# A graph-attention layer's preparation rewritten: plain fp32 projection, moments on VectorE, scores spread by DMA

## The chip, the cores and the metric

One NeuronCore of a Trainium2 chip runs the whole kernel. The metric is device time in microseconds (us), lower is better. The kernel before takes 437.5 us (median of 3 runs, 437.46 to 437.55).

Engine names as in the profile: PE is TensorE (matmul), PEld its weight loads, DVE is VectorE, ACT is ScalarE, POOL is GpSimd, SP is the queue that issues DMAs. Each engine runs its own instructions in order and waits on semaphores for the others.

## What is computed

```python
# x [4096, 256] f32, adj [4096, 4096] int32 (0.4 % ones), W1 [256, 256], b1, a1, a2 [256], b2 scalar
h   = relu(layernorm(x))                     # mean and variance of each row, eps 1e-5, no affine part
g   = h @ W1 + b1
e   = leaky_relu((g @ a1)[:, None] + (g @ a2)[None, :] + b2, 0.2)
att = softmax(where(adj > 0, e, -1e12), axis=1)
out = x + elu(att @ g)
```

The kernel never forms `e`. It uses exp(leaky(s1 + s2)) = exp(s2)·max(exp(s1 part), exp(s2 part)), so a weight is a maximum of two factors: R, which depends on the row i and is wanted along the free axis and repeated on all 128 partitions, and p, which depends on the neighbour j and sits one number per partition. A third factor u = exp(s2 - max) scales the rows of g.

## The kernel before

**Preparation.** The 4096 nodes are 32 tiles of 128, handled in 8 groups of 4 tiles (`GT`). For each group: `statistics` (4 `bn_stats` on VectorE), `moments` (7 tiny operations on GpSimd that turn them into mean and variance), `root` (ScalarE, square root), `invert` (VectorE, reciprocal and shift), `normalise` (2 of the 4 tiles on ScalarE, 2 on VectorE, into `xn`), `transposes` (8 on TensorE into PSUM banks 0 and 1), `relu_T` (ScalarE, PSUM to `hnT`, with a running sum in `hs`), `low_T` (VectorE, the rounding rest of `hnT`), `project` (TensorE: `W_hi·hnT + W_lo·hnT + W_hi·hnT_lo` in the fast fp32r format, 24 passes a group, into banks 2 to 5), `keep_h` (VectorE, PSUM plus bias to `h_raw`, in two halves). `exponents` (GpSimd) makes the arguments of the exponentials. For R, `repeat_s1` (ScalarE) repeats a group's 4 columns 128 times each, `spread` (TensorE) transposes them into PSUM banks 6 and 7, `keep_s` (ScalarE) copies them to R, and `exp_R` (ScalarE) takes the exponential 1024 columns at a time, one piece in each chunk of the main loop.

After the last group the maximum of s2 over all nodes is found (VectorE, TensorE, VectorE, TensorE, VectorE), `u` is made on ScalarE, the first two tiles of `hp_hi` and `hp_lo` follow, and TensorE starts the main loop. A small term `h_tiny`, 2^-100 times the sum of all h, is put into each accumulator by one matmul against `ones64` (`start_sum`), which covers rows with no neighbour.

**Main loop.** 4 chunks of 1024 output rows (8 PSUM banks of 128), each over 16 pairs of 128-node tiles. A pair is 1 MB of adjacency by DMA, then `sign` (ScalarE), `mask` (VectorE, two operations: max(R, p) times the sign), `high` (ScalarE, rounds to `w_hi`), `low` (VectorE, the rest `w_lo`), and 48 matmuls on TensorE: 32 of `w_hi` against `hp_hi` and `hp_lo`, then 16 of `w_lo` against `hp_hi`. In the first chunk the pairs' `hp_hi`, `hp_lo` are made on the way (`scale_h`, `round_h` on ScalarE, `low_h` on VectorE).

**What sets the order.** The instruction streams are written out by hand, one function for each engine, and meet at semaphores. Each engine's order around the change is the loop over `g` in its function. Two places are used by the prediction: VectorE's first `mask(0, 0, 0)`, which stands between two `keep_h`, and ScalarE's switch from the square-root table to the exponential table, which stands in front of its first exponential.

Of the kernel before, what the change touches and what calls it, by code (L numbers as in the profile page):

```python
# [32 lines left out]
P = 128  # L33
N = 4096
# [11 lines left out]
NORM_ACT = 2  # L46
# [6 lines left out]
EARLY = 6 * GT  # L53
# [27 lines left out]
def build(nc, adj_t, x, W1, vectors, out):  # L81
# [8 lines left out]
    with ctx:  # L90
# [37 lines left out]
        W_hi = sb("W_hi", [P, KC, HW], fp32r)  # L128
# [22 lines left out]
        cr = sb("cr", [P, TILES])  # L151
        cp = sb("cp", [P, TILES])
# [3 lines left out]
        H0, S0 = 2, 6  # L156
# [7 lines left out]
        pool_l = sem("pool_l")  # L164
        stat_ready = sem("stat_ready")
# [16 lines left out]
        s_kept = sem("s_kept")
# [10 lines left out]
        R_ready = sem("R_ready")  # L193
# [3 lines left out]
        eps_ready = sem("eps_ready")  # L197
        hp_tile = sem("hp_tile")
# [30 lines left out]
        def _(sp):  # L229
# [15 lines left out]
            for g in range(GROUPS):  # L245
                load_nodes(g)
                if g == 3:
                    load_adj(0, 0)
            for s in range(1, SLOTS):
                load_adj(s, s)  # L250

# [32 lines left out]
        def _(pool):  # L284
# [5 lines left out]
            links = [0]  # L290

            def link(ins):

                links[0] += 1
                ins.then_inc(pool_l, 1)
                pool.wait_ge(pool_l, links[0])

            def moments(g):

                pool.wait_ge(stat_ready, g + 1)  # L300
                st, mo = stats[:, g, :, :], mom[:, g, :, :]
                pool.tensor_tensor(mo[:, 0, :], st[:, :, 1], st[:, :, 4], ALU.add)
                pool.tensor_tensor(mo[:, 1, :], st[:, :, 1], st[:, :, 4], ALU.subtract)
                link(pool.tensor_tensor(mo[:, 2, :], st[:, :, 2], st[:, :, 5], ALU.add))
                pool.tensor_scalar(mean[:, g * GT:(g + 1) * GT], mo[:, 0, :], 0.5, None, ALU.mult)
                pool.tensor_tensor(mo[:, 3, :], mo[:, 1, :], mo[:, 1, :], ALU.mult)
                link(pool.tensor_scalar(mo[:, 2, :], mo[:, 2, :], 4.0 / F, None, ALU.mult))
                pool.tensor_tensor(var[:, g * GT:(g + 1) * GT], mo[:, 3, :], mo[:, 2, :], ALU.add).then_inc(var_ready, 1)

# [8 lines left out]
            for g in range(4):  # L318
                moments(g)
            pool.wait_ge(g3_ready, 1)  # L320
            for g in range(GROUPS):
                if g + 4 < GROUPS:
                    moments(g + 4)
                exponents(g)

# [7 lines left out]
        def _(act):  # L333
            act.dma_start(W1x[:, :, 0:F], W1.rearrange("(c p) f -> p c f", p=P)).then_inc(w_in, 16)
            act.dma_start(vec[:, :], vectors.partition_broadcast(P)).then_inc(vec_in, 16)

            def root(g):

                act.wait_ge(var_ready, g + 1)
                act.activation(std[:, g * GT:(g + 1) * GT], var[:, g * GT:(g + 1) * GT], ACT.Sqrt,  # L340
                               scale=0.25, bias=eps[:, 0:1]).then_inc(std_ready, 1)

            def normalise(g):

                act.wait_ge(rstd_ready, g + 1)
                if g >= 2:
                    act.wait_ge(tp_ready, KC * (g - 1))
                for t in range(NORM_ACT):
                    tile = g * GT + t
                    last = act.activation(xn[:, g % 2, t, :], x_s[:, tile, :], ACT.Identity,  # L350
                                          scale=rstd[:, tile:tile + 1], bias=shift[:, tile:tile + 1])
                last.then_inc(xn_act, 1)

            def relu_T(g):
# [559 lines left out]
```

## Time and profile before

| | us |
|---|---|
| median of 3 runs | 437.5 |
| the profiled execution's own time | 437.48 |
| its span in the trace | 435.7 |
| PE busy | 412.5 (95 %) |
| VectorE busy | 377.1 (87 %) |
| ScalarE busy | 315.9 (73 %) |
| GpSimd busy | 23.0 (5 %) |
| PE busy in 0 to 20 us | 6.5 |
| PE busy in 70 to 400 us | all of it |

The page's slices, each a fortieth of the span (10.9 us):

```profile
PE   0689979999999999999999999999999999999995
DVE  3999899999999389999996299999991799999925
ACT  2678899999996298957763798859562989586512
POOL 2333200000000000000000000000000000000003
```

A digit is the busy share of a slice in tenths. The preparation is the first five and a half slices, up to about 58 us; TensorE has gaps there and none from the seventh slice on. A busy share says nothing by itself about what an engine is worth, so the rows below give single starts and durations. The span is 1.8 us shorter than the device time of the same execution; that difference lies outside the trace.

### The profile page before, as it was taken

The numbers are of one execution on the slowest core, as the hardware profiler recorded it, in microseconds if no ns is written. First come the engines' busy times: TensorE is split into PE (matmuls) and PEld (weight loads), VectorE is DVE, ScalarE is ACT, GpSimd is POOL, SyncE is SP. The second block draws the span as 40 slices with busy tenths as digits, with TensorE's granted clock in tenths as the row PEclk, the third lists the DMA queues.
The fourth block names the chain that finished last, engine by engine and source line by source line (L and its number), as shares of the span: only waits on it lengthen the run. The fifth ranks groups of instructions, "written<-read, shape, count | busy, mean of one in ns | idle before, by whom it ended". The sixth has DMA issues, their size and how long they took to land.

```text
span 435.7 us, 8648 instructions
## 1 busy us (share of the span) xinstructions
PE 412.5 (95%) x3399; PEld 409.1 (94%) x3399; DVE 377.1 (87%) x404; ACT 315.9 (73%) x312; POOL 23.0 (5%) x94
## 2 busy tenths in 40 slices
PE   0689979999999999999999999999999999999995
PEld 0688979999999999999999999999999999999995
DVE  3999899999999389999996299999991799999925
ACT  2678899999996298957763798859562989586512
POOL 2333200000000000000000000000000000000003
PEclk9999999999999999999999999999999999999999
DMA  8940015556555725638478155647477256476202
GB/s 271 385 178 1 0 45 211 193 213 211 193 193 194 289 93 205 235 145 261 173 254 308 68 193 200 249 152 263 154 265 259 73 219 213 174 243 238 98 0 98
DMA packets 22360, 80.68 MB, mean 185 GB/s; under 512 B 1472, under 2 KB 14016, under 8 KB 14144
## 3 DMA queue, kind: packets, MB, share of 16 engines
q1 hardware_dynamic: 21920, 79.70, 52.1%
q10 hardware_dynamic: 416, 0.66, 0.5%
q8 instruction: 16, 0.26, 0.2%
q14 instruction: 8, 0.07, 0.0%
HBM read 76.15 MB, written 4.19 MB: 184 GB/s over the span
## 4 chain that ended last, share of the span: by engine, by line
PE 88%; DVE 7%; ACT 2%; DMA 2%; issue 0%; SPq 0%; DVEq 0%; ACTq 0%
PE ps L604 51%; PE ps L606 25%; PE ps L622 2%; PE ps L623 2%; PE ps L624 2%; DVE stats L664 2%; DMA x_s<-x 2%; DVE hnT_lo L691 1%; PE ps L531 1%; DVE h_raw L700 1%; PE ps L533 1%; PE ps L532 1%; DVE xn L681 1%; PE ps L580 1%; PE ps L519 1%; ACT h_raw L439 1%
## 5 line engine op out<-in xcount | busy, mean ns | idle before, releaser
L604 PE MATMUL ps<-hp_hi,w_hi 128*128 (+1 forms) x944 | 229.8, 282 | 0.9 <-ACT w_hi L391 0.9
L606 PE MATMUL ps<-hp_lo,w_hi 128*128 (+1 forms) x944 | 229.7, 282 | 0.0
L738 DVE SCALAR_TENSOR_TENSOR adj_s<-R,p,adj_s 128x1024 f32<-128x1024 f32 x128 | 158.1, 1275 | 31.7 <-ACT adj_s L383 31.7
L604 PEld LDWEIGHTS ps<-hp_hi,w_hi 128*128 128x128 f32 x944 | 178.3, 189 | 1.2 <-ACT w_hi L391 1.1
L606 PEld LDWEIGHTS ps<-hp_lo,w_hi 128*128 128x128 f32 x944 | 178.1, 189 | 0.0
L748 DVE SCALAR_TENSOR_TENSOR w_lo<-adj_s,w_hi 128x2048 fp32r<-128x2048 f32 x64 | 146.0, 2282 | 0.4 <-ACT w_hi L391 0.3
L391 ACT ACTIVATE w_hi<-adj_s 128x2048 fp32r<-128x2048 f32 x64 | 122.4, 1912 | 29.8 <-DVE adj_s L738 29.5
L383 ACT ACTIVATE adj_s<-adj_s 128x2048 f32<-128x2048 int32 x64 | 122.3, 1912 | 23.2 <-DMA adj_s<-adj_t 23.0
L604 PE MATMUL ps<-hp_hi,w_lo 128*128 (+1 forms) x944 | 123.1, 283 | 0.6 <-DVE w_lo L748 0.6
L604 PEld LDWEIGHTS ps<-hp_hi,w_lo 128*128 128x128 f32 x944 | 117.4, 189 | 0.8 <-DVE w_lo L748 0.8
L455 ACT ACTIVATE y<-ps 128x258 f32<-128x258 f32 x24 | 9.3, 387 | 27.9 <-PE ps L624 27.9
L330 POOL TENSOR_TENSOR adj_s<-y,adj_s 128x256 f32<-128x256 f32 x7 | 4.8, 692 | 372.9 <-DVE y L886 372.9
L519 PE MATMUL ps<-ident,xn 128*128 128x128 f32 x64 | 10.2, 312 | 15.1 <-ACT xn L350 11.3
L519 PEld LDWEIGHTS ps<-ident,xn 128*128 128x128 f32 x64 | 8.5, 161 | 15.8 <-issue 11.5
L622 PE MATMUL ps<-hp_hi,w_hi 128*128 128x258 f32 x80 | 22.6, 282 | 0.0
L623 PE MATMUL ps<-hp_lo,w_hi 128*128 128x258 f32 x80 | 22.6, 282 | 0.0
L624 PE MATMUL ps<-hp_hi,w_lo 128*128 128x258 f32 x80 | 22.5, 282 | 0.0
L531 PE MATMUL ps<-W_hi,hnT 128*128 128x258 f32 x64 | 19.1, 299 | 0.8 <-DVE h_raw L700 0.6
L532 PE MATMUL ps<-W_lo,hnT 128*128 128x258 f32 x64 | 18.3, 287 | 0.0
L533 PE MATMUL ps<-W_hi,hnT_lo 128*128 128x258 f32 x64 | 18.3, 286 | 0.0
L664 DVE BATCH_NORM_STATS2 stats<-x_s 128x6 f32<-128x256 f32 x32 | 11.2, 411 | 6.0 <-DMA x_s<-x 6.0
L623 PEld LDWEIGHTS ps<-hp_lo,w_hi 128*128 128x128 f32 x80 | 15.1, 189 | 0.0
(90 smaller groups left out, 270.2 us busy)
## 6 DMA issues: line engine op xcount, KB each, us to landing
adj_s<-adj_t SPq DMA_DIRECT2D x64, 1024.0 KB, 4.8
x_s<-x SPq DMA_DIRECT2D x8, 512.0 KB, 10.4
o_s<-x SPq DMA_DIRECT2D x3, 1024.0 KB, 7.5
out<-o_s SPq DMA_DIRECT2D x6, 512.0 KB, 6.8
adj_s<-x SPq DMA_DIRECT2D x1, 1024.0 KB, 5.3
out<-adj_s SPq DMA_DIRECT2D x8, 128.0 KB, 1.7
vec<-vectors ACTq DMA_DIRECT2D x1, 384.5 KB, 6.4
W1x<-W ACTq DMA_DIRECT2D x1, 256.0 KB, 4.3
```

The costliest lines, as they stand in the source:

```text
L383: act.activation(adj_w[:, c, :, :], adj_s[:, c, :, :], ACT.Sign).then_inc(signed, 1)
L391: act.activation(w_hi[:, c, :, :], adj_w[:, c, :, :], ACT.Relu).then_inc(hi_ready, 1)
L519: last = pe.transpose(ps[:, kc, t * P:(t + 1) * P], xn[:, u, t, kc * P:(kc + 1) * P], ident[:, :])
L531: pe.matmul(acc, hnT[:, u, kc, node], W_hi[:, kc, :], start=kc == 0, stop=False)
L532: pe.matmul(acc, hnT[:, u, kc, node], W_lo[:, kc, :], start=False, stop=False)
L604: last = pe.matmul(acc, block_w, hh, start=False, stop=False)
L606: pe.matmul(acc, block_w, hl, start=False, stop=False)
L622: pe.matmul(acc, w_hi[:, b + k, s, col], hh, start=False, stop=False)
L623: pe.matmul(acc, w_hi[:, b + k, s, col], hl, start=False, stop=False)
L624: last = pe.matmul(acc, w_lo[:, b + k, s, col], hh, start=False, stop=end)
L738: last = dve.scalar_tensor_tensor(sgn, R[:, ds(ic * CW, CW)], p[:, ds(source(r, c) + s, 1)], sgn, ALU.max, ALU.mult)
L748: dve.scalar_tensor_tensor(w_lo[:, c, :, :], adj_w[:, c, :, :], 0.0, w_hi[:, c, :, :].bitcast(fp32), ALU.max, ALU.subtract).then_inc(lo_re ...
```

## The change

Constants: `NORM_ACT` 2 to 3 (ScalarE normalises 3 of 4 tiles, 2 in the first two groups), `XN = 4` buffers for `xn`, `EARLY` 24 tiles to 16, `WARM = 19`.

- **Loads.** W1 and the vectors move from ScalarE's queue to SP's, behind group 0 of x; the first adjacency tile moves behind all of x.
- **Moments.** GpSimd's 7 operations go; VectorE runs 4 `bn_aggr` a group.
- **Projection.** `W_hi`, `W_lo`, `hnT_lo`, `split_weights` and `low_T` go. `project` is 8 plain fp32 matmuls a group. Transposes alternate between banks 0, 1 and 6, 7.
- **R.** `repeat_s1`, `spread`, `keep_s`, `exp_R` go. The scores are transposed once (8 tiles, then 24) into rows of PSUM, copied (`copy_r`), exponentiated as 8x128 and 24x128 (`exp_r`), written to a DRAM buffer and read back repeated on all partitions by DMA.
- **Start.** 19 fp32 matmuls of `ones` against `ones` ahead of the first transposes.
- **Tiny sums.** `start_sum` ahead of chunk 0 and at each chunk's start becomes `add_tiny` in the chunk's last pairs; the number of them is the same. `first_tile` opens the accumulators with `hp_hi` alone, then `hp_lo`.
- **Order of the first pairs.** On VectorE `low` of pair 0 stands ahead of `mask` of pair 1, and the first `mask` stands behind group 5 instead of behind group 6.

```diff
 # sync
-            for g in range(GROUPS):
+            load_nodes(0)
+            sp.dma_start(W1x[:, :, 0:F], ...); sp.dma_start(vec[:, :], ...)
+            for g in range(1, GROUPS):
                 load_nodes(g)
-                if g == 3:
-                    load_adj(0, 0)
+            load_adj(0, 0)
...
+            def spread(k):
+                a, b = R_PART[k]
+                sp.wait_ge(r_ready, k + 1)
+                sp.dma_start(r_rows[tiles, :], r_row[k][:, :]).then_inc(r_out, 16)
+                sp.wait_ge(r_out, (k + 1) * 16)
+                sp.dma_start(R[:, a * P:b * P],
+                             r_rows[tiles, :].rearrange("t p -> (t p)").partition_broadcast(P)).then_inc(R_in, 16)
 # scalar
+            def exp_r(k):
+                act.wait_ge(r_copied, k + 1)
+                act.activation(r_row[k][:, :], r_row[k][:, :], ACT.Exp).then_inc(r_ready, 1)
...
+            for g in range(2, GROUPS):
                 if g + 1 < GROUPS:
                     relu_T(g + 1)
                 if g + 3 < GROUPS:
                     root(g + 3)
+                    normalise(g + 3)
+                if g == 3:
+                    sign(0, 0, 0)
+                if g == 5:
+                    exp_r(0)
                     act.wait_ge(c_ready, EARLY // GT)
                     act.activation(p[:, 0:EARLY], cp[:, 0:EARLY], ACT.Exp).then_inc(p_ready, 1)
+                if g == 6:
+                    sign(0, 0, 1)
                     high(0, 0, 0)
+            exp_r(1)
 # tensor
+            def keep_warm(n):
+                for _ in range(n):
+                    pe.matmul(ps[:, H0 + GT - 1, 0:P], ones[:, :], ones[:, :], start=True, stop=True)
...
                     for kc in range(KC):
-                        pe.matmul(acc, hnT[:, u, kc, node], W_hi[:, kc, :], start=kc == 0, stop=False)
-                        pe.matmul(acc, hnT[:, u, kc, node], W_lo[:, kc, :], start=False, stop=False)
-                        last = pe.matmul(acc, hnT_lo[:, u, kc, node], W_hi[:, kc, :], start=False, stop=kc == KC - 1)
+                        last = pe.matmul(acc, hnT[:, g % 2, kc, node], W1x[:, kc, :], start=kc == 0, stop=kc == KC - 1)
...
+            transposes(0); project(0); transposes(1); project(1); transposes(2); project(2); transposes(3)
+            for g in range(3, GROUPS):
+                if g + 1 < GROUPS:
+                    transposes(g + 1)
+                if g == 4:
+                    turn_r(0)
+                project(g)                      # group 7: sum_h() after its second tile
+                if g == 4:
+                    pe.wait_ge(r_copied, 1)
 # vector
+                for t in range(GT):
+                    dve.bn_aggr(agg[:, g, t, :], stats[:, g, t, :]).then_inc(agg_ready, 1)
...
+            for g in range(2, GROUPS - 1):
+                if g + 3 < GROUPS:
+                    statistics(g + 3)
+                keep_h(g, (0,))
+                if g + 3 < GROUPS:
+                    invert(g + 3)
+                    normalise(g + 3)
                 if g == 4:
+                    copy_r(0)
+                keep_h(g, (1,))
+                if g == 5:
                     dve.wait_ge(p_ready, 1)
+                    dve.wait_ge(R_in, 16)
                     mask(0, 0, 0)
```

The order of VectorE's instructions around the first mask, before. `hnT_lo` is `low_T`, `h_raw` is `keep_h`, `hsrep` the repeated sums, `adj_s` the mask; the `h_raw` ahead of the mask is group 6, the one behind it group 7.

```order
L691 SCALAR_TENSOR_TENSOR hnT_lo<-ps,hnT 128x512 [waits hn_ready]
L700 TENSOR_TENSOR h_raw<-ps,b1x 128x516 [waits h_ready] x2
L782 TENSOR_REDUCE hsum<-hs 128x2 [waits hn_ready]
L784 TENSOR_SCALAR hsrep<-ones,hsum 128x128 [waits dve_c]
L784 TENSOR_SCALAR hsrep<-ones,hsum 128x128
L738 SCALAR_TENSOR_TENSOR adj_s<-R,p,adj_s 128x1024 [waits signed,R_ready,p_ready]
L738 SCALAR_TENSOR_TENSOR adj_s<-R,p,adj_s 128x1024
L700 TENSOR_TENSOR h_raw<-ps,b1x 128x516 [waits h_ready] x2
L792 TENSOR_REDUCE gm<-h_raw 128x1 [waits h_kept]
```

The same engine and place in the changed kernel. The three `h_raw` ahead of the mask are the second half of group 4 and both halves of group 5; the two behind it are group 6.

```order
L691 TENSOR_TENSOR h_raw<-ps,b1x 128x516 [waits h_ready]
L672 RECIPROCAL rstd<-std 128x4 [waits std_ready]
L673 SCALAR_TENSOR_TENSOR shift<-agg,rstd 128x4 [waits dve_c]
L682 TENSOR_SCALAR xn<-x_s,agg,rstd 128x256 [waits tp_ready]
L741 COPY r_row<-ps 8x128 [waits rT_ready]
L691 TENSOR_TENSOR h_raw<-ps,b1x 128x516 [waits h_ready] x3
L724 SCALAR_TENSOR_TENSOR adj_s<-R,p,adj_s 128x1024 [waits signed,R_in,p_ready]
L724 SCALAR_TENSOR_TENSOR adj_s<-R,p,adj_s 128x1024
L691 TENSOR_TENSOR h_raw<-ps,b1x 128x516 [waits h_ready] x2
L777 TENSOR_REDUCE hsum<-hs 128x2 [waits hn_ready]
```

The mask moved one group forward, and it now waits for `R_in`, the count of a DMA.

ScalarE in the changed kernel, from its last square root to the work behind the exponentials; `std` is `root(7)`, the two `hnT` pairs are `relu_T(6)` and `relu_T(7)`.

```order
L340 ACTIVATE std<-agg,eps 128x4 [waits agg_ready]
L349 ACTIVATE xn<-x_s,shift,rstd 128x256 [waits tp_ready,rstd_ready]
L349 ACTIVATE xn<-x_s,shift,rstd 128x256 x2
L359 ACTIVATE hnT,hs<-ps 128x512 [waits tp_ready,h_ready]
L359 ACTIVATE hnT,hs<-ps 128x512 [waits tp_ready]
L365 ACT_TABLE_LOAD
L365 ACTIVATE r_row<-r_row 8x128 [waits r_copied]
L406 ACTIVATE p<-cp 128x16 [waits c_ready]
L359 ACTIVATE hnT,hs<-ps 128x512 [waits tp_ready,h_ready]
L359 ACTIVATE hnT,hs<-ps 128x512 [waits tp_ready]
L370 ACTIVATE adj_s<-adj_s 128x2048 [waits adj_in1]
L378 ACTIVATE w_hi<-adj_s 128x2048 [waits masked]
```

The table switch and the first exponential stand behind `relu_T(6)`; before, they stood behind `relu_T(7)` and a `repeat_s1`, and R needed no DMA.

## Rows read from the trace of the kernel before

**Rows 1.** The page's chain of work that ended last, shares by engine.

```profile
PE 88%; DVE 7%; ACT 2%; DMA 2%; issue 0%; SPq 0%; DVEq 0%; ACTq 0%
```

**Rows 2.** Windows: stretch, length, busy us and instructions of PE, PEld, DVE, ACT, POOL.

```profile
70.00:80.00 10.00, 10.00 (x85) 10.00 (x85) 9.67 (x8) 10.00 (x12) 0.00 (x0) 1.00 0.54 197
```

**Rows 3.** Timeline of PE, end of preparation: start, us, instruction, idle before.

```profile
52.74 1.03 PE L568 MATMUL ps<-W1x,hsrep 128*128 128x256 f32 x4
53.60 0.60 PE L543 MATMUL ps<-ident,s1rep 128*128 128x128 f32 x4
...
65.68 0.39 PE L604 MATMUL ps<-hp_hi,w_hi 128*128 128x258 f32 x1 [0.88 <-ACT w_hi L391]
```

**Rows 4.** Timeline of PE, the first groups.

```profile
11.35 1.94 PE L519 MATMUL ps<-ident,xn 128*128 128x128 f32 x8 [11.35 <-ACT xn L350]
...
17.00 0.56 PE L531 MATMUL ps<-W_hi,hnT 128*128 128x258 f32 x1
...
22.32 1.07 PE L519 MATMUL ps<-ident,xn 128*128 128x128 f32 x8 [1.59 <-DVE xn L681]
```

**Rows 5.** Timeline of VectorE, one whole group in mid-preparation.

```profile
28.81 0.17 DVE L671 RECIPROCAL rstd<-std 128x4 f32<-128x4 f32 x1
...
29.09 1.29 DVE L691 SCALAR_TENSOR_TENSOR hnT_lo<-ps,hnT 128x512 fp32r<-128x512 f32 x2
30.30 0.73 DVE L681 TENSOR_SCALAR xn<-x_s,mean,rstd 128x256 f32<-128x256 f32 x2
30.94 1.40 DVE L664 BATCH_NORM_STATS2 stats<-x_s 128x6 f32<-128x256 f32 x4
32.26 1.28 DVE L700 TENSOR_TENSOR h_raw<-ps,b1x 128x516 f32<-128x516 f32 x2
```

**Rows 6.** Timeline of ScalarE, sign, relu_T, normalise and root.

```profile
31.40 1.90 ACT L383 ACTIVATE adj_s<-adj_s 128x2048 f32<-128x2048 int32 x1
33.20 0.58 ACT L360 ACTIVATE hnT<-ps 128x512 fp32r<-128x512 f32 x1
...
34.34 1.09 ACT L350 ACTIVATE xn<-x_s,shift,rstd 128x256 f32<-128x256 f32 x2
35.32 0.29 ACT L340 ACTIVATE std<-var,eps 128x4 f32<-128x4 f32 x1
```

**Rows 7.** Timeline of ScalarE, the table switch.

```profile
48.16 1.28 ACT L415 ACT_TABLE_LOAD   x1
49.45 0.22 ACT L415 ACTIVATE p<-cp 128x24 f32<-128x24 f32 x1
```

**Rows 8.** Timeline of VectorE, first mask and maximum.

```profile
50.82 2.48 DVE L738 SCALAR_TENSOR_TENSOR adj_s<-R,p,adj_s 128x1024 f32<-128x1024 f32 x2
...
54.54 0.21 DVE L792 TENSOR_REDUCE gm<-h_raw 128x1 f32<-128x32 f32 x1
```

**Rows 9.** Timeline of ScalarE, from the first hp_hi on.

```profile
56.54 0.91 ACT L433 ACTIVATE hp_hi<-h_raw,u 128x258 fp32r<-128x258 f32 x2
...
58.16 1.06 ACT L374 ACTIVATE R<-ps 128x512 f32<-128x512 f32 x2
59.26 0.64 ACT L446 ACTIVATE hp_hi<-h_raw 128x516 fp32r<-128x516 f32 x1
```

**Rows 10.** The page's costliest groups, one row: busy, mean ns, idle before.

```profile
L748 DVE SCALAR_TENSOR_TENSOR w_lo<-adj_s,w_hi 128x2048 fp32r<-128x2048 f32 x64 | 146.0, 2282 | 0.4 <-ACT w_hi L391 0.3
```

**Rows 11.** The page's DMA issues: KB each, median us to landing.

```profile
adj_s<-adj_t SPq DMA_DIRECT2D x64, 1024.0 KB, 4.8
...
out<-adj_s SPq DMA_DIRECT2D x8, 128.0 KB, 1.7
```

**Rows 12.** Timeline of VectorE, first statistics and weights.

```profile
5.32 1.41 DVE L664 BATCH_NORM_STATS2 stats<-x_s 128x6 f32<-128x256 f32 x4 [4.37 <-DMA x_s<-x]
...
10.64 0.28 DVE L707 COPY b1x<-vec 128x256 f32<-128x256 f32 x1
...
12.35 0.21 DVE L715 TENSOR_SCALAR W1x<-w1a 128x1 f32<-128x1 f32 x2
```

More of the change, by code:

```diff
@@ L45 @@
 GROUPS = TILES // GT
-NORM_ACT = 2
+NORM_ACT = 3
+PAIRED = 2
+WARM = 19
+XN = 4
+R_CUT = CW // P
+R_PART = ((0, R_CUT), (R_CUT, TILES))
 HW = F + 2
@@ L289, in _ @@
                                pattern=[[-1, P]], channel_multiplier=1).then_inc(pool_c, 1)
[L290 to L308, printed above, removed]
+            pool.memset(ones64[:, :].bitcast(fp32), 1.0 / 64).then_inc(h_sum_set, 1)
+            pool.memset(h_sum[:, F:F + 1], float(N)).then_inc(h_sum_set, 1)
+            pool.memset(h_sum[:, F + 1:HW], 0.0).then_inc(h_sum_set, 1)
             def exponents(g):
@@ L480, in round_of @@
                         sign(*ahead(ic, r, c, 2))
-                    if r is FIRST_ROUND and c == 2 and not last:
-                        exp_R(ic + 1)
                     if inner and not first and c in (1, 2):
@@ L564, in _, with turn_r @@
-            project(GROUPS - 1, 1)
-            pe.wait_ge(hsrep_ready, 1)
-            for kc in range(KC):
-                last = pe.matmul(ps[:, 0, 0:F], hsrep[:, kc, :], W1x[:, kc, 0:F], start=kc == 0, stop=kc == KC - 1)
-            last.then_inc(hsum_ps, 1)
-            spread(GROUPS - 2, 0)
+                    if g == GROUPS - 1 and t == 1:
+                        sum_h()
+            def turn_r(k):
+                a, b = R_PART[k]
+                pe.transpose(ps[0:b - a, RB[k], 0:P], cr[:, a:b], ident[:, :]).then_inc(rT_ready, 1)
@@ new lines, in sum_h @@
+            def sum_h():
+                pe.wait_ge(hsrep_ready, 1)
+                for kc in range(KC):
+                    last = pe.matmul(ps[:, 0, 0:F], hsrep[:, kc, :], W1x[:, kc, 0:F], start=kc == 0, stop=kc == KC - 1)
+                last.then_inc(hsum_ps, 1)
+            pe.wait_ge(pool_c, 1)
+            keep_warm(WARM)
+            pe.wait_ge(pool_c, 3)
+            transposes(0)
+            pe.wait_ge(w1x_ready, 1)
+            project(0)
+            transposes(1)
+            project(1)
@@ L587, in pair @@
                     for s in range(2):
+                        if first and begin and part == 0 and s == 0:
+                            first_tile()
+                            continue
                         if first and part == 0:
@@ L804, in _ @@
-            rest = slice(P // 2, P)
-            dve.wait_ge(tiny_ready, 1)
-            dve.scalar_tensor_tensor(h_tiny[rest, :], h_sum[rest, :], TINY, h_tiny[rest, :].bitcast(fp32),
-                                     ALU.mult, ALU.subtract).then_inc(prep_done, 1)
+            dve.wait_ge(hn_ready, GROUPS * KC)
+            link(dve.reduce_sum(hsum[:, :], hs[:, :, :], AX.X))
+            for kc in range(KC):
+                last = dve.tensor_scalar(hsrep[:, kc, :], ones[:, :], hsum[:, kc:kc + 1], None, ALU.mult)
@@ L839, in round_of @@
                     end = last and r is LAST_ROUND
-                    if not (end and c == SLOTS - 1):
+                    begin = first and r is FIRST_ROUND and c == 0
+                    if not (end and c == SLOTS - 1) and not begin:
                         mask(*ahead(ic, r, c, 1))
                     low(ic, r, c)
+                    if begin:
+                        mask(*ahead(ic, r, c, 1))
                     if first and not (r is LAST_ROUND and c == SLOTS - 1):
                         low_h(*ahead(ic, r, c, 1)[1:])
+                    if first and r is FIRST_ROUND and c == 2:
+                        tiny()
                     if r is FIRST_ROUND and c == 3 and not first:
```

321 lines of the change are left out of this document (141 added, 180 removed).

## The prediction, made before the changed kernel was run

> **What bounds the kernel now.** I read the chain of waits first: 88 % of it is TensorE [rows 1]. Then the windows by time: from 70 us on TensorE is busy in all of every stretch, at 85 matmuls in 10 us, which is 0.118 us each [rows 2]. Then TensorE's own timeline for the last place where it waits: pair 1 of the first chunk starts at 65.68 after 0.88 us of idle [rows 3]. Behind that point nothing but TensorE counts, and its matmuls are the same in both kernels. So the change is worth what it moves the start of pair 1, plus any matmul that it moves from ahead of that point to behind it. I call the end of the last projection X. It is 52.74 before, where the sum of h starts directly behind it [rows 3], and pair 1 starts 12.94 later.
>
> **Costs of the parts, per group.** The plain fp32 projection: the two fp32 matmuls of the h sum leave four records, 0.86 us from their start to the next instruction [rows 3], so 0.215 a record and 0.43 a matmul of 256 columns. A group has 8: 3.44 us. Before it had 24 passes at 0.118: 2.83. With eight transposes (0.9; their rows say 1.07 with the last one's tail [rows 4]) TensorE needs 4.3 us a group. VectorE before: starts at 28.81, 29.09, 30.30, 30.94, 32.26 and 1.2 for the last give 4.65 a group [rows 5]. It loses low_T (1.21) and one of two xn (0.32) and gains four bn_aggr and a link. No row shows bn_aggr. The nearest are tiny operations: 0.06 to 0.10 each as the second of two in a row (12.35, two in 0.21 [rows 12]), 0.17 busy as a reciprocal [rows 5]. That bounds four and a link between 0.3 and 0.8; I take 0.45, near the short end because the four do not wait for each other. VectorE: 3.6. ScalarE: two relu_T 1.14, root 0.2, three xn at 0.5 each [rows 6]: 2.85. By these sums TensorE would set the pace at 4.3. The order says otherwise, so I walk it.
>
> **The walk.** P0 to P7 are the starts of the eight projections. x's first group: 5.32 before [rows 12]; now no other load shares its first microsecond, so 4.6 (bounds 4.0 and 5.3). Statistics, bn_aggr, root, reciprocal, shift: 7.2. ScalarE's two xn: 8.3. Transposes 8.5 to 9.4, at the fast level: the 19 fp32 matmuls of ones end shortly before. Before, the first eight took 1.94 and later ones 1.07 [rows 4]; that halving is 1.2 against 2.4 GHz. The weights take VectorE 1.9 (10.64 to 12.35 plus 0.21 [rows 12]) and end at 9.7; relu_T(0) ends at 10.4. P0 = 10.5, against 17.00 before [rows 4]: 6.5 us ahead.
>
> P1 = 16.1: P0 ends at 14.0, transposes of group 1 only then, relu_T behind them.
> P2 = 23.2, not 20.4. P1 ends at 19.55, the transposes at 20.45, relu_T(2) on ScalarE at 21.5; root(3) stands behind it (21.8), VectorE waits for that root before keep_h(1), and P2 needs the banks that keep_h(1) frees (0.6 for reciprocal and xn, 0.7 for the half). TensorE idles 2.8.
> P3 = 30.1, not 27.5. VectorE has from 23.65: statistics and moments of 4 (1.8), root (0.35), invert and xn (0.6), the scalars (1.2: two of the four reductions of rows 12 and two linked tiny operations), statistics of 5 (1.8), a half of keep_h(2) (0.65), in all 6.4.
> P4 = 34.7. P3 ends at 33.6, one set of transposes.
> P5 = 40.7, not 39.1. ScalarE from 34.0: three xn 1.5, sign 1.8, relu_T(5) 1.2, root(7) 0.3, so VectorE's invert(7), xn and copy_r(0) end at 39.7, and the next transposes wait for that copy.
> ScalarE goes on: xn(7) to 40.75, relu_T(6) to 41.95, the table switch 1.3 to 43.25 [rows 7], exp_r to 43.5.
>
> **The new wait.** R's first columns now come over two DMAs in a row. The write of 4 KB: 1.7, as the 128 KB stores [rows 11]. The repeated read of 512 KB: the 1 MB load takes 4.8 [rows 11]; two points on a line, 128 KB in 1.7 and 1024 KB in 4.8, give 3.0, and I add 0.2 for 128 repeats: 3.2 (bounds 2.4, half of 4.8, and 4.8). R is in at 48.5. VectorE has been standing in front of mask(0,0,0) since keep_h(5) at 45.0. Queued behind it: the mask, 2.4 [rows 8], then keep_h(6), for whose banks the last projection waits. TensorE ends P6 at 48.5 and starts P7 at 48.5 + 0.05 + 2.4 + 0.7 = 51.65. The wait and the mask thus cost TensorE 3.1 us. Counted from P5 it is tight: relu_T(6) 1.25, table 1.3, exp 0.25, two DMAs 4.9, mask and half 3.1 give P5 + 10.9, while TensorE alone could start P7 at P5 + 7.8.
> P7 takes 3.44 and the h sum in its middle 0.86: X = 55.95, against 52.74.
>
> The Trainium skill, "ScalarE: Activation LUTs", section "What ACT_TABLE_LOAD costs", puts a switch at about 2.66 us, a load of 1283 ns and a drain of 1380 ns. The trace agrees with the load (1.28) and not with the drain: the next activation starts 1.29 after the load's start [rows 7]. By the page's rule R would be in 1.4 us later, and the time 441.0; I go by the row.
>
> **From X to pair 1.** The maximum starts at X + 0.45, now straight from PSUM; before, the first mask and both halves of keep_h held it until 54.54 [rows 8], X + 1.8. From the maximum to the first hp_hi it was 2.00 (54.54 to 56.54 [rows 8, 9]); the same steps remain, so X + 2.45. From there to pair 1 ScalarE took 9.14 (56.54 to 65.68 [rows 3, 9]). It loses two copies to R, 1.10 (58.16 to 59.26 [rows 9]), and gains a tiny exponential, 0.2: 8.2, so X + 10.7. VectorE gets there at about the same time by the other way: keep_h(7) to X + 3.2, two hp_lo 0.9, low 2.2 [rows 10], mask 2.4 [rows 8], then high 1.9: X + 10.9, since low now stands ahead of the mask. I take 10.9. Low of pair 0 is thereby early, which buys nothing by itself: TensorE waits for pair 1's high all the same.
> Pair 1 starts at 55.95 + 10.9 = 66.85, 1.15 later than before. Eight tiny matmuls of chunk 0 that stood in waiting time ahead of pair 1 now stand in the saturated stretch: 8 × 0.118 = 0.95. From there on the work for pairs 2 to 4 comes 0.5 us or more ahead of TensorE by the same durations, and the second read of R, 1.5 MB ahead of the adjacency loads in SP's queue, is wanted only at the chunk's end.
>
> **Sum.** 437.48 (the profiled execution, 435.7 of span and 1.8 outside; the median is 437.50, the same) + 1.15 + 0.95 = 439.6. The 6.5 us won at P0 go to: P2 2.8, P3 2.6, P5 1.6, R's wait 3.1, and the slower fp32 projection.
>
> **Rivals.**
> A. The early groups run at TensorE's own pace: ScalarE and VectorE catch up, no stall at P2, P3, P5. Then P5 = 10.5 + 1.2 + 5 × 4.3 = 33.2, P7 = 44.1, X = 48.4, pair 1 at 59.3: 437.5 - 6.4 + 0.95 = 432.1. For it: VectorE's sum of 3.6 is below 4.3. Against it: the root behind relu_T is a circle through three engines, and rows 5 show before that VectorE in order is what sets the pace.
> B. The other side, by R's trip: place, the wait in front of mask(0,0,0). If both DMAs together take 1.7 instead of 4.9, R is in by 45.2, the stall shrinks from 3.6 to nothing, X = 52.75 and pair 1 starts at 63.65: 437.5 - 2.0 + 0.95 = 436.4. Equality with before is reached at a trip of 2.8. For it: the write is only 4 KB. Against it: no DMA in the rows lands in under 1.7, and there are two, one waiting for the other.
> C. The clock. TensorE has gaps of 2.8 (ahead of P2) and 3.1 (ahead of P7), longer than the 1.59 ahead of a fast burst [rows 4]. If it falls to 1.2 GHz there, a projection takes up to 3.4 more, some of which the R wait absorbs: 439.6 + 1 to 4, so about 442. The Trainium skill, "TensorE: Matmul & The Clock Gate", says the clock is halved after an idle stretch and given back by sustained work; the trace agrees in that the first work ran at half speed. None of the rows shows a fast engine falling back after a gap of this length.
> D. bn_aggr at its long bound, 0.35 more in each of seven groups on VectorE's path: 2 later, 441.7.
>
> **How the numbers follow.** My walk with small errors 0.48, A 0.08, B (a short trip, or the walk too slow by 2 to 4 in front) 0.17, C 0.15, D 0.12. No change within what a measurement can tell is 0.2 %, 0.9 us: 436.6 to 438.4. Faster: A, B's larger part and a little of the walk: 0.23. Same: a part of the walk and of B: 0.17. Slower: 0.60. The range leaves A out below and the worst of C above: 436.2 to 442.8. The likeliest case alone: 438.3 to 441.
>
> **What the next profile would show.** Right: P0 at 10 to 11; a gap on TensorE of 2 to 3 ahead of P2; VectorE idle about 3.5 in front of the first mask, released by a DMA; no idle of TensorE behind pair 1; pair 1 at 66 to 67. Wrong: no idle at the mask (then B), TensorE without gaps from P1 to P5 (then A), transposes of 1.9 us after P1 (then C). The whole forecast falls if TensorE idles anywhere behind pair 1, or if fp32 passes take other than 0.215.

## The result, and the profile after

The changed kernel took a median of 441.53 us (eight runs, 439.45 to 443.24) against 437.56 for the kernel before (437.43 to 437.68): 1.0085 times the time [1.0063, 1.0106], so 4.0 us slower. The forecast was 439.6 with a range to 442.8: the sign is right, the range holds, and the value is 1.9 short. It lies outside the narrower interval of the likeliest case (438.3 to 441). The spread is new too: single executions lay 3.8 us apart, against 0.25 before.

The profiled execution took 442.08, and one subtraction tells where the time is. Pair 1 starts at 69.17 instead of 65.68 [rows 3]: 3.49 later. From its start to the end of the span it is 371.13 instead of 370.02: 1.11 more. 437.48 + 3.49 + 1.11 = 442.08. TensorE has no idle time behind that start up to 400 us, as before [rows 2]; windows, columns as there but for TensorE alone (length, busy and matmuls, granted clock, DMA share, GB/s):

```profile
100.00:400.00 300.00, 300.00 (x2504) 1.00 0.59 205
```

So everything of interest lies ahead of 69.17. The page's chain answers to [rows 1]; its clock line has a dip in the second tenth of the span, and none behind it:

```profile
PE 87%; DVE 4%; ACT 4%; DMA 3%; issue 1%; SPq 0%; DVEq 0%; ACTq 0%
PEclk9999889999999999999999999999999999999999
```

TensorE's timeline answers to [rows 3, 4]: start, us, instruction, and in brackets the idle time ahead and what ended it. L517 with 16 records is one group's projection. P0 is the row at 10.76; of P6 and P7 see the rows at 45.08 and 52.47.

```profile
10.76 3.75 PE L517 MATMUL ps<-W1x,hnT 128*128 128x258 f32 x16 [1.60 <-DVE W1x L706]
16.37 3.75 PE L517 MATMUL ps<-W1x,hnT 128*128 128x258 f32 x16 [0.92 <-ACT hnT L359]
...
23.59 3.73 PE L517 MATMUL ps<-W1x,hnT 128*128 128x258 f32 x16 [2.59 <-DVE h_raw L691]
30.41 3.72 PE L517 MATMUL ps<-W1x,hnT 128*128 128x258 f32 x16 [1.14 <-DVE h_raw L691]
...
39.78 1.09 PE L505 MATMUL ps<-ident,xn 128*128 128x128 f32 x8 [1.18 <-DVE r_row L741]
40.71 3.65 PE L517 MATMUL ps<-W1x,hnT 128*128 128x258 f32 x16
...
45.08 3.65 PE L517 MATMUL ps<-W1x,hnT 128*128 128x258 f32 x16
...
52.47 3.55 PE L517 MATMUL ps<-W1x,hnT 128*128 128x258 f32 x8 [3.74 <-DVE h_raw L691]
55.82 1.18 PE L532 MATMUL ps<-W1x,hsrep 128*128 128x256 f32 x4
56.84 1.90 PE L517 MATMUL ps<-W1x,hnT 128*128 128x258 f32 x8
...
69.17 0.39 PE L604 MATMUL ps<-hp_hi,w_hi 128*128 128x258 f32 x1
```

Read the brackets from top to bottom. P0 really is 6.2 us ahead of before, and P1 even 7.4 (23.80 before). The brackets ahead of P2 (2.59), P3 (1.14) and the transposes for P5 (1.18) take most of that back, and the largest one, 3.74, ahead of P7, takes the rest and more. Before, in the same places, two starts to compare with:

```profile
28.44 0.36 PE L531 MATMUL ps<-W_hi,hnT 128*128 128x258 f32 x1 [0.22 <-DVE h_raw L700]
...
49.78 0.36 PE L531 MATMUL ps<-W_hi,hnT 128*128 128x258 f32 x1
```

The first is P2, the second P7: the changed kernel is 4.9 us ahead at the one and 2.7 behind at the other. Read then the second column of the two halves of P7: eight records take 3.55 in the first half and 1.90 in the second. That is the clock (columns as above; the granted clock, the third number, is the share of TensorE's full speed, 1.00 for 2.4 GHz and 0.50 for 1.2):

```profile
49.00:52.00 3.00, 0.00 (x0) 1.00 0.00 0
52.00:54.00 2.00, 1.53 (x4) 0.68 0.00 0
54.00:56.00 2.00, 2.00 (x6) 0.50 0.00 0
56.00:58.00 2.00, 2.00 (x11) 0.97 0.00 0
```

TensorE stood idle to 52.47, fell from 2.4 to 1.2 GHz as it began again, and had nearly the full clock again in the last of these windows. The projection's first half pays 1.65 for it, and the h sum's start the rest.

VectorE's timeline around the new wait, where [rows 8] had the first mask start at 50.82:

```profile
44.40 0.70 DVE L691 TENSOR_TENSOR h_raw<-ps,b1x 128x516 f32<-128x516 f32 x1 [1.05 <-PE ps L517]
49.24 2.48 DVE L724 SCALAR_TENSOR_TENSOR adj_s<-R,p,adj_s 128x1024 f32<-128x1024 f32 x2 [4.13 <-DMA R<-r_rows]
51.63 1.29 DVE L691 TENSOR_TENSOR h_raw<-ps,b1x 128x516 f32<-128x516 f32 x2
```

VectorE is done with group 5 at 45.1, stands 4.13 us in front of the mask, and only behind the mask comes `keep_h(6)`, whose banks P7 needs. The chain in order of time (start, us, what) shows what it waits for: the switch to the exponential's table, the exponential of R's row, and the two transfers one behind the other:

```profile
42.00 1.28 ACT L365
...
43.29 0.32 ACT r_row L365
...
43.62 1.22 DMA r_rows<-r_row
...
44.86 4.28 DMA R<-r_rows
```

### The profile page after: what moved, and what is told of

It is laid out like the page before. It is cut to its first block, busy times and chain, and to the rows that moved or that the text cites. A ratio compares the mean times of both kernels' runs of the same rounds, so it can differ in the third digit from the quotient of the medians.

```text
span 440.3 us, 8443 instructions
## 1 busy us (share of the span) xinstructions
PE 420.8 (96%) x3343; PEld 413.1 (94%) x3343; DVE 367.8 (84%) x415; ACT 308.9 (70%) x300; POOL 10.7 (2%) x39
## 4 chain that ended last, share of the span: by engine, by line
PE 87%; DVE 4%; ACT 4%; DMA 3%; issue 1%; SPq 0%; DVEq 0%; ACTq 0%
PE ps L604 51%; PE ps L606 25%; PE ps L517 3%; PE ps L625 2%; PE ps L624 2%; PE ps L626 2%; DMA vec<-vectors 2%; ACT hnT L359 1%; DMA R<-r_rows 1%; DVE stats L663 1%; PE ps L566 1%; DVE h_raw L691 1%; ACT adj_s L370 1%; DVE adj_s L724 1%; ACT h_raw L423 1%
## 5 line engine op out<-in xcount | busy, mean ns | idle before, releaser
L604 PEld LDWEIGHTS ps<-hp_hi,w_hi 128*128 128x128 f32 x936 | 177.6, 190 | 0.3 <-ACT w_hi L378 0.3
L604 PEld LDWEIGHTS ps<-hp_hi,w_lo 128*128 128x128 f32 x944 | 117.4, 189 | 0.0
L517 PE MATMUL ps<-W1x,hnT 128*128 128x258 f32 x128 | 31.4, 398 | 10.0 <-DVE h_raw L691 7.5
L517 PEld LDWEIGHTS ps<-W1x,hnT 128*128 128x128 f32 x128 | 24.5, 196 | 14.8 <-issue 8.3
L624 PEld LDWEIGHTS ps<-hp_hi,w_hi 128*128 128x128 f32 x80 | 15.1, 189 | 0.0
L626 PEld LDWEIGHTS ps<-hp_hi,w_lo 128*128 128x128 f32 x80 | 15.1, 189 | 0.0
L489 ACT ACTIVATE y<-ps,rden 128x256 f32<-128x256 f32 x8 | 3.8, 474 | 15.6 <-DVE rden L883 15.6
L349 ACT ACTIVATE xn<-x_s,shift,rstd 128x256 f32<-128x256 f32 x22 | 11.7, 591 | 3.9 <-DVE shift L673 3.9
```

The source lines that it names most:

```text
L349: last = act.activation(xn[:, g % XN, t, :], x_s[:, tile, :], ACT.Identity, scale=rstd[:, tile:tile + 1], bias=shift[:, tile:tile + 1])
L517: last = pe.matmul(acc, hnT[:, g % 2, kc, node], W1x[:, kc, :], start=kc == 0, stop=kc == KC - 1)
L604: last = pe.matmul(acc, block_w, hh, start=fresh, stop=False)
L624: pe.matmul(acc, w_hi[:, b + k, s, col], hh, start=False, stop=False)
L626: last = pe.matmul(acc, w_lo[:, b + k, s, col], hh, start=False, stop=end)
```

## The experiments

Nine more kernels were run beside the kernel before, which took 437.55 to 437.58 in all of them. Two numbers of each profile are used throughout: the start of pair 1, and the tail, from there to the end of the span.

### 1. The first mask behind the last projection's work (e1_mask_late)

The changed kernel, with the wait for R and the mask behind the h sum's operand, so behind `keep_h(6)`:

```diff
                 keep_h(g, (1,))
-                if g == 5:
-                    dve.wait_ge(p_ready, 1)
-                    dve.wait_ge(R_in, 16)
-                    mask(0, 0, 0)
...
             last.then_inc(hsrep_ready, 1)
+            dve.wait_ge(p_ready, 1)
+            dve.wait_ge(R_in, 16)
+            mask(0, 0, 0)
```

> The first mask and its wait for R move behind keep_h(6) and the repeated sums; nothing else changes. Theory 1 (the wait for R's two DMAs in front of keep_h(6) holds the last projection, and the clock that falls in that gap slows it): R lands at 49.2 as in the changed kernel, no gap of TensorE ahead of the last projection, it starts at 48.7 and all its passes run at the fast level, X = 53.0, pair 1 at 63.5, time 436 to 436.8. Theory 2 (the slower fp32 projection and the stalls of the early groups are the loss, the wait for R only covers other waits): pair 1 stays at 68 to 69 and the time at 440 to 442.

Measured: 436.92 (436.2 to 439.08, ten runs), 0.999 of before [0.9978, 1.0002]: no clear difference from before, and 4.6 us below the changed kernel. Pair 1 starts at 64.08, 5.1 earlier; the tail is 371.12, the same. TensorE's timeline, then VectorE's:

```profile
45.65 5.40 PE L517 MATMUL ps<-W1x,hnT 128*128 128x258 f32 x24
...
51.74 1.90 PE L517 MATMUL ps<-W1x,hnT 128*128 128x258 f32 x8
```

```profile
50.54 2.48 DVE L724 SCALAR_TENSOR_TENSOR adj_s<-R,p,adj_s 128x1024 f32<-128x1024 f32 x2
```

P7 follows P6 without a gap (24 records in one row), at the full clock, and the mask waits for nothing: R was in before it was wanted. The R trip itself is harmless here; what cost the time is the place of the wait for it. Of the 5.1 between the two profiles, 3.3 lie ahead of P7 (its start is 49.1 here, 52.47 there) and 1.8 between P7's start and X (4.3 here, 6.1 there), which is the clock.

One row of this profile has the low clock in an earlier place. P2 stands behind the same gap as in the changed kernel, with the same instructions ahead of it, and took 5.18 instead of 3.73:

```profile
23.53 5.18 PE L517 MATMUL ps<-W1x,hnT 128*128 128x258 f32 x16 [2.59 <-DVE h_raw L691]
```

Most of that disappeared in the stall ahead of P3; P5 was 0.6 later (41.28 instead of 40.71).

### 2. The gap filled, the wait kept (e2_gap_filled)

This parts the wait from the clock that fell behind it. The changed kernel with 16 matmuls of ones (32 records) while TensorE waits for P7:

```diff
+                if g == GROUPS - 1:
+                    keep_warm(16, 1)
                 project(g)
```

> 16 plain fp32 matmuls of ones (about 3.4 us at the fast level) into a free bank fill TensorE's gap ahead of the last projection; the wait for R stays. Theory 1 with the clock as a term of its own: the last projection starts at 52.5 as before, takes 4.3 in place of 6.1, X = 56.9, pair 1 at 67.4, time 440.0 to 440.6, and the runs lie closer together than the 3.8 us of the changed kernel. Theory 3 (the slow passes are not from the gap, or are hidden behind ScalarE anyway): 441 to 442, the same spread.

Measured: 440.48 (439.81 to 442.23, four runs), 1.0061 [1.0044, 1.0077], 1.05 below the changed kernel. The projection behind the filled gap is fast again, while VectorE still waits for R:

```profile
50.77 3.73 PE L496 MATMUL ps<-ones 128*128 128x128 f32 x32
54.34 1.91 PE L517 MATMUL ps<-W1x,hnT 128*128 128x258 f32 x8
```

```profile
50.66 2.48 DVE L726 SCALAR_TENSOR_TENSOR adj_s<-R,p,adj_s 128x1024 f32<-128x1024 f32 x2 [3.37 <-DMA R<-r_rows]
```

In the profiles this parts the two: X minus P7's start is 4.3 here and 6.1 in the changed kernel, so the slow clock at P7 was worth 1.8 in that execution, and the wait the rest. For the medians it does not: the intervals overlap ([1.0063, 1.0106] there), so the 1.05 is not shown to be more than noise. The filling also cost something of its own. P7 starts 3.68 behind the mask's start, 3.23 in the changed kernel, since the ones ran some 0.45 too long. The profiled execution was the slowest of the four, and it shows the same thing in other gaps that this kernel leaves open. Its first projection, behind a gap of 1.49, took 5.44 instead of 3.75, and P2 5.20 instead of 3.73; the windows have the clock at 0.66 and 0.69 there:

```profile
10.69 5.44 PE L517 MATMUL ps<-W1x,hnT 128*128 128x258 f32 x16 [1.49 <-DVE W1x L708]
...
25.14 5.20 PE L517 MATMUL ps<-W1x,hnT 128*128 128x258 f32 x16 [2.60 <-DVE h_raw L693]
```

```profile
10.00:15.00 5.00, 4.31 (x12) 0.66 1.10 362
...
25.00:30.00 5.00, 4.86 (x16) 0.69 0.46 190
```

### 3. The fp32 projection alone (e3_fp32_alone)

The kernel before, with only this:

```diff
-                        pe.matmul(acc, hnT[...], W_hi[:, kc, :], ...)
-                        pe.matmul(acc, hnT[...], W_lo[:, kc, :], ...)
-                        last = pe.matmul(acc, hnT_lo[...], W_hi[:, kc, :], ...)
+                        last = pe.matmul(acc, hnT[...], W1x[:, kc, :], start=kc == 0, stop=kc == KC - 1)
...
-            split_weights()
-            low_T(0)
```

> The kernel before with one part of the change alone: plain fp32 projection, no low_T, no split weights. Theory 1: VectorE loses 1.2 us a group and 1.1 at the start, TensorE gains 0.6 a group (0.9 + 3.44 + 0.44 for the spread = 4.8 against a pace of 4.65 before): the two cancel to 1 us, time 437 to 438.7. Theory 2 (the fp32 projection is the loss): 439.5 or more.

Measured: 437.89 (437.16 to 438.61, ten runs), 1.0005 [0.9995, 1.0015]: no difference. Pair 1 at 66.16, tail 370.04. The groups follow at 4.80:

```profile
27.20 3.65 PE L531 MATMUL ps<-W1x,hnT 128*128 128x258 f32 x16
...
32.00 3.65 PE L531 MATMUL ps<-W1x,hnT 128*128 128x258 f32 x16
```

VectorE's 4.65 a group became TensorE's 4.80 (the rows say 3.65 for 16 records at 0.215 each because the last record's tail is in them). Taking work off VectorE gave back nothing, since the same edit gave it to TensorE.

### 4. Without the warm-up (e4_no_warm)

`WARM = 19` to `WARM = 0` in the changed kernel.

> The changed kernel without the 19 matmuls of ones. Theory 1 (the chain P0, P1, root(3), keep_h(1), P2 passes every delay on): the first transposes take 1.9 in place of 1.1, P0's first passes 0.43 each in place of 0.22, P1 starts 2 to 3 later and so does all behind it, time 443 to 445. Rival: the 2.6 us gap ahead of P2 and the later ones absorb it, time within 1 us of the changed kernel's 441.5.

Measured: 443.01 (442.33 to 443.81, four runs), 1.013 [1.0113, 1.0147], 1.5 slower than the changed kernel, at the low edge of what was expected. The start runs at half speed:

```profile
8.32 1.94 PE L505 MATMUL ps<-ident,xn 128*128 128x128 f32 x8 [8.32 <-ACT xn L349]
11.13 5.60 PE L517 MATMUL ps<-W1x,hnT 128*128 128x258 f32 x16 [0.87 <-ACT hnT L359]
...
54.38 1.98 PE L517 MATMUL ps<-W1x,hnT 128*128 128x258 f32 x8 [2.93 <-DVE h_raw L691]
```

P0 is 1.9 longer and P5 2.7 later, but pair 1 in the profile only 0.2 later (69.40). Not all of the 2.7 is the missing warm-up: P2 took 5.13 here too, behind its gap of 2.59. The last row shows where the 2.7 went besides the wait: here P7 came out of a gap of 2.93 at full speed, where the changed kernel, behind 3.74, fell to half. The 0.2 is thus a matter of two single executions; the medians differ by 1.5.

### 5. The tiny matmuls left out (e5_tiny_out)

Experiment 1's kernel, without chunk 0's eight tiny matmuls; this leaves the tiny sum out of chunk 0.

```diff
-                    add_tiny(ib)
+                    if not first:
+                        add_tiny(ib)
```

> e1 with the eight tiny matmuls of chunk 0 left out (rows without a neighbour in the first 1024 lose their small term). The term of my sum: eight matmuls in the saturated stretch, 8 x 0.118 = 0.95 us less than e1, 435.9 to 436.2 by median. Rival: TensorE has slack there (ScalarE or VectorE sets the pace behind pair 1) and nothing changes: 436.9.

Measured: 435.82 (435.33 to 437.36, six runs), 0.9964 [0.9952, 0.9977]. The median is 1.1 below experiment 1's, and the tail, which the clock of the preparation can't touch, fell from 371.12 to 370.11. That is 1.0 of the 1.1 by which the tail had grown from before, so nothing else of the change costs more than 0.1 behind pair 1.

### 6. The front stalls taken out (e6_front_only)

The changed kernel; on VectorE `keep_h(1)` no longer stands behind the root of group 3 nor the scalars behind group 4's work, and on ScalarE the first sign stands behind the first exponentials:

```diff
             statistics(3)
+            scalars()
+            keep_h(1)
             invert(3)
             normalise(3)
-            keep_h(1)
             statistics(4)
...
-            scalars()
...
-                if g == 3:
-                    sign(0, 0, 0)
...
                     act.activation(p[:, 0:EARLY], cp[:, 0:EARLY], ACT.Exp).then_inc(p_ready, 1)
+                    sign(0, 0, 0)
```

> The changed kernel with three moves in the early groups and the mask where the change put it: keep_h(1) ahead of invert(3), the scalars into VectorE's 3 us wait for root(3), sign(0,0,0) from ahead of relu_T(5) to behind the first exponentials. Theory 1 (the stalls ahead of P2, P3 and P5 are order on VectorE and ScalarE, and everything behind P5 hangs on P5): P2 at 22.0, P5 at 37.2 in place of 40.7, the wait for R as long as before, time 438.0 (437.5 to 438.7). Rival (R's trip or another engine's sum is a floor of its own): 440 or more.

Measured: 437.4 (435.34 to 439.64, twelve runs), 0.9996 [0.9979, 1.0013], so 4.1 below the changed kernel and 0.1 below the expected range. P2 starts at 21.55 instead of 23.59, P5 at 36.77 instead of 40.71, pair 1 at 66.03. The profiled execution, 438.98, is 1.6 above the median. The wait for R is untouched, and in this execution the clock falls behind it:

```profile
44.75 2.48 DVE L723 SCALAR_TENSOR_TENSOR adj_s<-R,p,adj_s 128x1024 f32<-128x1024 f32 x2 [3.60 <-DMA R<-r_rows]
```

```profile
47.98 3.78 PE L516 MATMUL ps<-W1x,hnT 128*128 128x258 f32 x8 [3.20 <-DVE h_raw L690]
```

### 7. Both (e7_both)

Experiments 1 and 6 together.

> e1's mask and e6's three moves together. Theory 1: the two gains add, X = 49.5, pair 1 at 60, time 433.4 (432.8 to 434.2), below the kernel before by 4. Rival: R lands too late for the mask behind the repeated sums, and takes 1 to 3 us back: 434.5 to 436.5.

Measured: 432.73 (432.31 to 434.48, five runs), 0.9899 [0.9885, 0.9913]. The two gains add: 4.6 and 4.1 make 8.7, measured 8.8. Pair 1 starts at 59.39:

```profile
40.97 5.40 PE L516 MATMUL ps<-W1x,hnT 128*128 128x258 f32 x24
...
59.39 0.39 PE L603 MATMUL ps<-hp_hi,w_hi 128*128 128x258 f32 x1 [1.57 <-ACT w_hi L378]
```

Pair 1 is where rival A had it (59.3), but not by rival A's way. A had P5 at 33.2 and the wait for R left in, so P7 at 44.1; here P5 starts at 36.60, with gaps of about 1 ahead of P0, P1 and P2, and P7 follows P6 without a wait, at 44.5. That the two agree at pair 1 is chance.

### 8. And the other gaps filled (e8_gaps_filled)

Experiment 7's kernel with 6, 3, 5 and 6 matmuls of ones ahead of P0, P1, P2 and the first pair:

```diff
             transposes(0)
+            keep_warm(6)
             pe.wait_ge(w1x_ready, 1)
             project(0)
             transposes(1)
+            keep_warm(3, 1)
             project(1)
             transposes(2)
+            keep_warm(5, 7)
             project(2)
...
             def first_tile():
+                pe.wait_ge(r_copied, 2)
+                keep_warm(6, RB[1])
                 pe.wait_ge(hi_ready, 1)
```

> e7 with plain fp32 matmuls of ones in four gaps of TensorE: 6 ahead of P0, 3 ahead of P1, 5 ahead of P2, 6 ahead of the first pair (each about 0.22 us at the fast level). Theory 1 with the clock as the cause of the spread: fewer stretches at the half clock, spread of the runs under 1 us in place of 3, median lower than e7's by 0.2 to 0.6. Rival (the spread comes from elsewhere, or the fills push the real work back): the same spread, median equal or higher.

Measured: 432.5 (432.46 to 433.01, four runs), 0.9888 [0.9874, 0.9902]. The mean granted clock of the profiled execution is 1.000 and the runs lie 0.55 apart, where experiment 7's lie 2.2 and the changed kernel's 3.8. The median moved by 0.23 only, which is inside the intervals. Experiment 7's 2.2 is one execution of five: 434.48, at a mean granted clock of 0.990, where its other four have 0.996 to 0.999 and lie 0.6 apart. This fits the clock in the gaps ahead of pair 1 as a large part of the spread, and does not show it: four runs are few, and experiment 3's ten runs lie 1.45 apart at 0.999 to 1.000, so there is a source besides.

### 9. The tiny matmuls back into waiting time (e9_tiny_in_wait)

Experiment 8's kernel; `h_tiny` is made on GpSimd, and chunk 0's eight tiny matmuls stand ahead of pair 1:

```diff
+            pool.tensor_scalar(h_tmp[:, :], h_sum[:, :], TINY, None, ALU.mult)
+            pool.tensor_scalar(h_tiny[:, :], h_sum[:, :], TINY, None, ALU.mult).then_inc(tiny_ready, 1)
+            pool.wait_ge(tiny_ready, 1)
+            pool.tensor_tensor(h_tiny[rest, :], h_tmp[rest, :], ..., ALU.subtract).then_inc(prep_done, 1)
...
+                if m == 1:                      # ahead of pair 1
+                    for ib in range(BANKS):
+                        add_tiny(ib)
```

> e8 with chunk 0's eight tiny matmuls moved into TensorE's wait of 1.6 us ahead of pair 1, and h_tiny made on GpSimd instead of VectorE. Theory 1 (matmuls in the saturated stretch cost 0.12 each, in a wait nothing): 1.0 us less than e8, 431.4 to 431.7, and 370.1 us from pair 1 to the end of the span in place of 371.2. Rival (GpSimd is too slow or VectorE's share of the time was worth something): GpSimd's three operations take over 7 us and pair 1 starts later, 432 or more; or more than 1.3 us less, if the 0.7 of VectorE counted.

Measured: 432.36 (431.87 to 432.57, four runs), 0.9879 [0.9862, 0.9895]: no clear gain over experiment 8, a miss. The tail did shrink, from 371.1 to 370.03, but pair 1 came 0.84 later:

```profile
58.16 1.12 PE L577 MATMUL ps<-h_tiny,ones 128*128 128x258 f32 x8
...
60.47 0.39 PE L620 MATMUL ps<-hp_hi,w_hi 128*128 128x258 f32 x1 [1.19 <-ACT w_hi L387]
```

The tiny matmuls are not what delays it: there is 1.19 of idle time behind them. VectorE's low of pair 0 took 2.84, where experiment 8's took 2.28. First GpSimd beside it, then VectorE, then VectorE of experiment 8:

```profile
52.11 0.88 POOL L332 TENSOR_SCALAR h_tiny<-h_sum 128x258 fp32r<-128x258 f32 x1
53.08 0.86 POOL L335 TENSOR_TENSOR h_tiny<-h_tmp,h_tiny 64x258 fp32r<-64x258 f32 x1
```

```profile
53.24 2.84 DVE L750 SCALAR_TENSOR_TENSOR w_lo<-adj_s,w_hi 128x2048 fp32r<-128x2048 f32 x1
```

```profile
52.96 2.28 DVE L737 SCALAR_TENSOR_TENSOR w_lo<-adj_s,w_hi 128x2048 fp32r<-128x2048 f32 x1
```

That accounts for 0.56 of the 0.84. The other 0.28 were there before low began (53.24 against 52.96), and they arose ahead of anything that the edit touches: P0 itself started at 10.71 instead of 10.41, since VectorE's wait for the vectors ended 0.30 later in this execution (8.72 against 8.42). That GpSimd causes the longer low is argued from these rows; no run kept it off GpSimd with all else the same.

## Why the forecast was right, and where its value was off

Starts in the walk and in the changed kernel's profile:

| | walk | measured | before |
|---|---|---|---|
| P0 | 10.5 | 10.76 | 17.00 |
| P1 | 16.1 | 16.37 | 23.80 |
| P2 | 23.2 | 23.59 | 28.44 |
| P3 | 30.1 | 30.41 | 32.99 |
| P4 | 34.7 | 34.95 | 37.86 |
| P5 | 40.7 | 40.71 | 42.26 |
| P6 | 45.1 (its end, 48.5, less 3.44) | 45.08 | 46.45 |
| R in | 48.5 | 49.18 | |
| P7 | 51.65 | 52.47 | 49.78 |
| X | 55.95 | 58.6 | 52.74 |
| pair 1 | 66.85 | 69.17 | 65.68 |
| tail, more than before | 0.95 | 1.11 | |

**What held.** That nothing but TensorE counts behind pair 1: no idle time there, and tails that agree to 0.1 us in all kernels with the same matmuls. The stalls ahead of P2, P3 and P5 (2.59, 1.14 beside the late transposes, 1.18), each released by the instruction that the walk named; experiment 6 shows them to be an order of instructions and no lack of speed, worth 4.1 us. The new wait in front of the mask, by experiment 1. The tiny term, forecast at 0.95 and measured at 1.0 to 1.1 (experiments 5 and 9). P0 was 0.26 late because the vectors came late: VectorE stood 1.26 us for them ahead of the weights.

**What was mis-sized.** Two terms of the step on the last projection, and one behind it:
- R's trip. Forecast 1.7 + 3.2; measured 1.22 + 4.28, 5.5 with the links. The line through two loads gave 3.2 for a read of 512 KB, and the repeated read took 1.1 more; the short write gave 0.5 back. With 0.1 at the exponentials and 0.1 at the mask this put P7 0.8 late. But the 4.28 is the highest of nine profiles: in experiments 1, 2 and 4 to 9 the same read took 3.4 to 3.8, so the trip was 4.7 to 5.0 there and the forecast's 4.9 is about right. What missed in this execution is a term that varies.
- The clock. X minus P7 was forecast as 3.44 + 0.86 = 4.3 and was 6.1. That is rival C's mechanism, at P7, which had a chance of 0.15 and no share in the sum. It is 1.8 us in the profiled execution; its size in the median one was not measured (experiment 2).
- X to pair 1 was 10.55 instead of 10.9. This is a slip in the sum: the terms that the forecast lists for VectorE's way, 3.2 + 0.9 + 2.2 + 2.4 + 1.9, make 10.6, and the 10.9 has 0.3 that no term stands for.

Together 0.8 + 1.8 - 0.35 = 2.3, the whole difference at pair 1 (69.17 - 66.85); with 0.16 of the tail the profiled execution is 2.5 above the forecast. Without the slip it would be 2.8, so that part of the closeness is luck.

The forecast said of rival C that no row showed a fast engine falling back after a gap of that length. That was true, and it was read too much as evidence that it doesn't: the kernel before had only one such gap, of 1.59, ahead of work that is easily timed. Rival C's time, about 442, is nearer to the 441.53 than the sum's 439.6. By the Trainium skill, "TensorE: Matmul & The Clock Gate", section "HAM oscillation — how this bites in real kernels", a kernel whose TensorE stops and starts moves between the two levels. Experiment 2 agrees, with 5.44 against 3.75 behind a gap of 1.49; experiment 4 shows that a gap need not do it, with full speed behind 2.93.

**The rivals.** A is false for this kernel (TensorE had its gaps), and in experiment 7 too P5 came at 36.60 and not at 33.2. B is false: the trip took 4.7 to 5.5 in all profiles, where B had 1.7 and equality with before 2.8. C happened in part: at P7, and not ahead of P2 in this execution; its sign, transposes of 1.9 after P1, did not appear. D is false: the four `bn_aggr` took 0.38 together, so 0.45 with their link was right:

```profile
5.68 0.38 DVE L666 BATCH_NORM_AGGREGATE agg<-stats 128x2 f32<-128x6 f32 x4
```

**What stays open.** When exactly the clock falls: gaps of 1.5 to 3.7 us did it in some executions and not in others of like length, and no run varied the gap alone. What the clock and R's trip cost in the median execution was not measured either; only profiled ones have starts. And no run took the new loads, the `bn_aggr` or R's trip alone into the kernel before.

A version exists that beats both kernels. Experiments 7 to 9 take 432.4 to 432.7, 1.1 % below before and 2 % below the changed kernel: all of the rebuilt preparation, with `keep_h(1)` ahead of the wait for root(3), `keep_h(6)` ahead of the wait for R, and the first sign behind the first exponentials.

## What to carry to other kernels

Find the last place where the bounding engine still waits, and price a change by what it does to that instant, plus what it moves behind it: here a start that was 6.2 us earlier ended 3.5 us later, and 1.1 us of matmuls had left their waiting time. A wait costs what is queued behind it in order: put the instructions that free a buffer for the bounding engine ahead of any wait for something slower, above all for two DMAs in a row. Where a change opens gaps on TensorE, count its next burst once at half clock as the upper end of that term, and watch the spread of the runs; matmuls of ones can fill a gap that can't be closed, as long as they end before the real work is ready. Read the size of a transfer from more than one profile: R's first read alone moved by 0.9 us between executions.

## What the hardware showed that was not expected

- The clock fell behind short gaps, and not each time. The changed kernel and experiments 1, 2 and 5 have the same instructions up to P2, and behind the same gap of 2.59 to 2.60 P2 ran at full speed in two of the profiles and not in the other two. Each cell has the idle time ahead and how long the projection then took (us):

| profile | P0 | P2 | P7, first half |
|---|---|---|---|
| changed kernel | 1.60, 3.75 | 2.59, 3.73 | 3.74, 3.55 |
| experiment 1 | 1.46, 3.75 | 2.59, 5.18 | no gap |
| experiment 2 | 1.49, 5.44 | 2.60, 5.20 | filled, 1.91 |
| experiment 4 (no warm-up) | 0.87, 5.60 | 2.59, 5.13 | 2.93, 1.98 |
| experiment 5 | 1.87, 5.37 | 2.59, 3.73 | no gap |
| experiment 6 | 1.04, 3.75 | 0.98, 3.75 | 3.20, 3.78 |

  Ahead of P0 and P2 eight transposes stand just before the gap, ahead of P7 a projection; whether that matters was not tested.
- A read of 4 KB repeated onto 128 partitions (512 KB in all) took 4.28 us in the changed kernel's profile, nearly as long as the plain 1 MB load [rows 11], and 3.4 to 3.8 in the eight others that have it. The rest of R, three times as much, took 6.2 (6.1 to 8.3 in the others). The page's DMA issues (KB each, median us to landing):

```profile
R<-r_rows SPq DMA_DIRECT2D x1, 1536.0 KB, 6.2
R<-r_rows SPq DMA_DIRECT2D x1, 512.0 KB, 4.3
```

- A GpSimd operation of 0.86 us with two inputs came with 0.56 us more for VectorE's two-input operation beside it (2.84 instead of 2.28). GpSimd's one-input operation just ahead (52.11 to 52.99) ran beside VectorE's two `hp_lo`, which took 0.48 each with it and without it. The Trainium skill, "GPSIMD Engine Reference", section "Specifications", says that GpSimd shares its interfaces to the memory with VectorE and contends with instructions that have two inputs there. The trace agrees for the one low; the two `hp_lo` have two inputs as well and show nothing.
